# The shift of a softmax's scores: minima split in token layout, turned in f32r one step later, and written to the queries straight from PSUM

## The chip, the core and the metric

The kernel runs on one core of a Trainium2 chip. The metric is the time on the device in microseconds, the median of several executions. Matrix products run on TensorE (PE in the rows, its weight loads PEld), elementwise work on VectorE (DVE), ScalarE (ACT) and GpSimd (POOL); SyncE (SP) issues most DMAs. Every engine works through its own list of instructions in order, and engines wait for each other by semaphores.

## The reference

Two batches of 512 tokens of width 512 attend to 1,024 context tokens each, in 16 heads of 32. The first 257 context tokens ("image") and the other 767 ("text") have separate key and value weights and **separate softmaxes**, whose results are added:

```
q = rms_norm(linear(x, q_w, q_b)); k, k_img likewise from the context
img_x = softmax(q k_img^T / sqrt(32)) v_img
txt_x = softmax(q k^T / sqrt(32)) v
x = x + linear(txt_x + img_x, o_w, o_b)
```

A feed-forward stage follows: the last token of each batch goes four times through a 512-2048-512 layer with GELU, and its result, under a sigmoid gate of every token, is added and normalised.

## The kernel before

**Units and steps.** Attention runs over 16 units: 2 halves of the queries x 2 batches x 4 groups of 4 heads, 256 queries each. A unit has 8 steps of 128 keys. The function `make_plan` (line 69) writes one list of steps out by hand, and every engine goes through it and does its own part of each; so the list sets the order on all engines. In step r of the loop of line 247 TensorE does

- `S2(r)`: scores of step r with the keys on partitions and 4 x 256 (head, query) columns, four f32r products (line 837);
- `PV(r-1)`: probabilities times values of the step before, in f32 (line 856, with row sums on line 861);
- `S1(r+12)`: scores of a unit one and a half ahead, now with the queries on partitions, two f32r products of 512 columns (line 820). They serve to find maxima alone. VectorE reduces them to negated maxima `negt` (lines 1273 and 1275); three PSUM banks take turns.

In between stand pieces of the rest: output projection (`o`), the feed-forward chain (`ch_...`), the gate (`f_...`).

**The shift.** exp needs the scores less a maximum per query, head and softmax. The maximum is added inside S2: the operands `kst` and `qst` have 112 rows, of which 96 hold keys and queries (split in high and low f32r parts) and 16 hold, in `kst`, ones at the right (head, image or text) and in `qst` the negated maxima, in 8 rows the high and in 8 the low part. They get there so:

1. `maxes(u)`, VectorE (line 1279): two small minima over the partial results give `negm`, 128 queries x 16, the 8 values twice, in f32.
2. `shift(u)`, TensorE (line 881): two f32 products with the identity turn it to 16 x 256 in rows 96 to 111 of a PSUM bank.
3. `shift(u)`, ScalarE (line 1102): copy to `crow` in f32r, which rounds to the high part. `shift(u)`, VectorE (line 1298): high rows stay, low rows become value minus high part, by a column `lows` of 0 and -1 that a DMA brings.
4. `spread(u)`, ScalarE (line 1108): the 16 rows are copied to the four heads of `qst`.

Units are counted from 0 in the code (u) and from the first in the text: the ninth unit is u = 8. The minima and the shift of unit u stand in step 4 of unit u-1, that is between S1 and the next S2, and the spread in step 5; S2 of unit u needs them three steps later. Unit 0 is done in the first phase, between the value projections.

## Time and profile before

| | |
|---|---|
| median of 3 runs | 564.36 us (559.66 to 565.49) |
| the profiled execution's own time | 565.07 us |
| its span, first to last instruction | 563.2 us |
| TensorE busy, of the span | 519.2 us, 92% |
| VectorE, ScalarE, GpSimd busy | 64%, 55%, 41% |
| mean granted TensorE clock | 0.969 |

The first 155 us are projections, the last 45 us gate and output; between them the 16 units run at 17.5 us each where nothing else stands among their steps. The page gives shares of the whole span. What a change inside a unit is worth is read from the timeline of one step: which engine another one waits for there, and how far apart the groups of one engine start.

### The profile page before, as it was taken

What the parts mean: (1) busy time and instruction counts of PE and PEld (TensorE: products, weight loads), DVE (VectorE), ACT (ScalarE), POOL (GpSimd) and SP (SyncE); (2) the same over time, 40 slices, a digit from 0 to 9 for tenths busy, and PEclk for the clock granted to TensorE, in tenths of its full rate; (3) what the DMA queues carried; (4) which work ended last, traced back from release to release, by engine and by line L of the source; (5) the groups of instructions that cost most, each with busy time, mean ns of one, the idle gap of its engine ahead of it and who ended that gap; (6) DMA issues with size and microseconds to landing.
All of it is one profiled execution on the core that took longest, in us unless ns stands there. A gap on an engine that the chain in (4) does not pass through costs nothing.

```text
span 563.2 us, 9907 instructions
## 1 busy us (share of the span) xinstructions
PE 519.2 (92%) x3800; PEld 318.4 (57%) x3800; DVE 358.9 (64%) x760; ACT 310.3 (55%) x556; POOL 233.5 (41%) x140
## 2 busy tenths in 40 slices
PE   4999999599898999999999999999999999998970
PEld 3888879477664555555556454445454545554430
DVE  4388666667676478567766687384747375439565
ACT  4874367232265466446666364657474646767432
POOL 1230022220075385545546427070716164849531
PEclk9999999889999799999999997999999999999995
DMA  8977379829889969746777685425242363000101
GB/s 297 402 224 275 149 169 259 236 84 309 221 246 278 219 154 245 200 133 174 201 202 199 127 225 162 126 57 127 57 127 58 125 189 118 2 20 19 39 19 56
DMA packets 61328, 91.92 MB, mean 163 GB/s; under 512 B 4513, under 2 KB 29105, under 8 KB 60705
## 3 DMA queue, kind: packets, MB, share of 16 engines
q1 hardware_dynamic: 56848, 74.68, 47.8%
q0 software_dynamic: 3312, 14.51, 7.8%
q10 hardware_dynamic: 1120, 2.10, 1.3%
q8 instruction: 30, 0.49, 0.4%
q14 instruction: 18, 0.14, 0.1%
HBM read 71.87 MB, written 19.66 MB: 163 GB/s over the span
## 4 chain that ended last, share of the span: by engine, by line
PE 67%; DVE 15%; DMA 8%; ACT 4%; POOL 3%; issue 3%; SPq 0%; POOLq 0%; DVEq 0%; ACTq 0%
PE psum L747 12%; PE psum L856 11%; PE psum L820 10%; PE psum L837 9%; PE psum L861 6%; PE psum L895 5%; DMA qscr<-hl 3%; DVE negt L1275 3%; PE psum L932 3%; DVE negt L1273 2%; PE psum L756 2%; PE psum L952 2%; DMA qst<-qscr 2%; PE psum L988 2%; PE psum L884 2%
## 5 line engine op out<-in xcount | busy, mean ns | idle before, releaser
L1090 ACT ACTIVATE prob<-psum 128x512 f32<-128x512 f32 x256 | 138.5, 593 | 99.4 <-PE psum L837 97.2
L1275 DVE TENSOR_REDUCE negt<-psum 128x1 f32<-128x512 f32 (+1 forms) x256 | 134.9, 548 | 55.0 <-PE psum L820 54.7
L1505 POOL TENSOR_TENSOR added<-added,prob 128x1024 f32<-128x1024 f32 x48 | 114.2, 2380 | 14.8 <-ACT prob L1090 9.5
L820 PE MATMUL psum<-kst,qst 96*128 96x512 f32 x256 | 98.9, 462 | 12.8 <-DVE negt L1275 9.2
L1502 POOL TENSOR_TENSOR added<-prob 128x1024 f32<-128x1024 f32 x16 | 38.0, 2372 | 154.6 <-ACT prob L1090 154.6
L837 PE MATMUL psum<-qst,kst 112*128 112x256 f32 x512 | 94.0, 301 | 1.2 <-ACT prob L1090 0.8
L837 PEld LDWEIGHTS psum<-qst,kst 112*128 112x128 f32 x512 | 77.8, 192 | 28.3 <-ACT prob L1090 10.2
L856 PE MATMUL psum<-prob,vring 128*32 128x256 f32 x1152 | 90.7, 397 | 0.0
L820 PEld LDWEIGHTS psum<-kst,qst 96*128 96x128 f32 x256 | 40.7, 190 | 66.9 <-issue 36.8
L1273 DVE TENSOR_REDUCE negt<-psum 128x1 f32<-128x257 f32 x128 | 53.0, 414 | 30.4 <-PE psum L820 30.3
L1455 POOL TENSOR_TENSOR ssum<-sq 128x512 f32<-128x512 f32 x6 | 8.6, 1439 | 80.1 <-ACT sq L1055 63.8
L861 PE MATMUL psum<-prob,ones 128*32 128x256 f32 x512 | 36.9, 383 | 0.0
L856 PEld LDWEIGHTS psum<-prob,vring 128*32 128x32 f32 x1152 | 24.7, 109 | 20.7 <-issue 1.1
L1054 ACT ACTIVATE raw<-psum,colp 128x512 f32<-128x512 f32 (+2 forms) x32 | 19.1, 596 | 29.7 <-PE psum L747 28.3
L747 PE MATMUL psum<-p_wv,tok 128*128 128x512 f32 x144 | 34.4, 392 | 0.0
L988 PE MATMUL psum<-wg,xTt 128*128 128x512 f32 x64 | 30.2, 607 | 0.6 <-ACT xTt L1158 0.6
L747 PEld LDWEIGHTS psum<-p_wv,tok 128*128 128x128 f32 x144 | 26.9, 188 | 5.9 <-issue 0.2
L895 PE MATMUL psum<-wbuf,attT 128*128 128x512 f32 x64 | 29.4, 601 | 0.4 <-issue 0.4
L747 PE MATMUL psum<-tok,p_wk 128*128 128x256 f32 (+1 forms) x144 | 25.9, 331 | 0.0
L1072 ACT ACTIVATE vbuf<-psum 128x512 f32<-128x512 f32 x14 | 8.4, 598 | 29.6 <-PE psum L747 29.5
L747 PEld LDWEIGHTS psum<-tok,p_wk 128*128 128x128 f32 x144 | 22.2, 198 | 2.4
L747 PE MATMUL psum<-tok,p_wq 128*128 128x512 f32 x96 | 23.5, 400 | 0.0
(159 smaller groups left out, 683.5 us busy)
## 6 DMA issues: line engine op xcount, KB each, us to landing
kst<-kscr SPq DMA_DIRECT2D x96, 256.0 KB, 5.7
vring<-vscr SPq DMA_DIRECT2D x16, 576.0 KB, 7.0
kscr<-hl SPq DMA_DIRECT2D x16, 512.0 KB, 2.9
d<-d POOLq DMA_DIRECT2D x8, 1024.0 KB, 6.9
qst<-qscr SPq DMA_DIRECT2D x48, 128.0 KB, 5.6
vscr<-vbuf SPq DMA_DIRECT2D x18, 256.0 KB, 2.7
qscr<-hl SPq DMA_DIRECT2D x8, 512.0 KB, 5.0
in_c<-ctxT SPq DMA_DIRECT2D x2, 1024.0 KB, 12.4
```

Of the source, the lines that this page charges most:

```text
L747: mm = pe.matmul(ps, left(a, kc), right(b, kc), start=(kc == 0 and a + b == 0), stop=(kc == KC - 1 and a == 1))
L820: pe.matmul(psum[:, n % 3, :], qst[0:96, slot, jj, qt * P:(qt + 1) * P], kst[0:96, slot, jj, half * 512:(half + 1) * 512], start=True, sto ...
L837: mm = pe.matmul(score2[:, j * QH:(j + 1) * QH], kst[0:96 + 4 * HPG, slot, jj, k0:k0 + P], qst[0:96 + 4 * HPG, slot, jj, :], start=True, s ...
L856: mm = pe.matmul(psum[32 * j:32 * j + 32, PV_BANK, st * QH:(st + 1) * QH], vring[:, u % 2, vc, 32 * j:32 * j + 32], prob[:, r % NP, j * QH ...
L861: mm = pe.matmul(psum[32 * j:32 * j + 32, SUM_BANK, st * QH:(st + 1) * QH], ones[:, kind, :], source[:, j * QH:(j + 1) * QH], start=first, ...
L895: mm = pe.matmul(ps, attT[:, g, n * P:(n + 1) * P], wbuf[:, g, :], start=(g == 0), stop=(g == NG - 1))
L988: mm = pe.matmul(ps, xTt[:, f % 2, kc, :], wg[:, kc, :], start=(kc == 0), stop=(kc == KC - 1))
L1090: act.activation(prob[:, r % NP, part], score2[:, part], ACT.Exp).then_inc(exp2_done, 1)
L1273: dve.tensor_reduce(negt[:, u % 2, qt, 0, j:j + 1], psum[:, n % 3, 0:IMG], AX.X, ALU.max, negate=True)
L1275: dve.tensor_reduce(negt[:, u % 2, qt, half, HPG + j:HPG + j + 1], psum[:, n % 3, k0:512], AX.X, ALU.max, negate=True)\
L1502: pool.tensor_tensor(added[:, :], prob[:, (r - 1) % NP, :], prob[:, r % NP, :], ALU.add).then_inc(added_done, 1)
L1505: pool.tensor_tensor(added[:, :], added[:, :], prob[:, r % NP, :], ALU.add).then_inc(added_done, 1)
```

## The change

- The negated maxima are split where the queries are still on partitions. `maxes` writes the high part to `negm`, now f32r and 112 columns wide (columns 0 to 95 are zero, written once), then the value and the negated high part to `negp`, and their sum as low part to `negm`: four small instructions, the third and fourth each waiting for one before it.
- TensorE turns `negm` with an f32r identity, so that its 112 columns are the weights and the output takes rows 0 to 111.
- The ScalarE copy to `crow` and VectorE's subtraction go; `spread` reads PSUM itself. The bank is free when `spread` is done.
- In the loop `shift` stands one step later, between S2 and PV.
- The DMA of `lows` goes; a copy makes the f32r identity in unit 0.

```diff
     for r in range(8 * NU + 2):
         if r < 8 * NU:
             add('S2', r)
+            if (r + ahead) % 8 == 1 and r + ahead <= 8 * NU + 1:
+                add('shift', (r + ahead) // 8 - 1)
...
         if t < 8 * NU:
             add('S1', t)
-        if t % 8 == 0 and t <= 8 * NU:
-            add('shift', t // 8 - 1)
...
-        negm = sb("negm", [P, 2, 2, 4 * HPG], F32, o); o += 256
+        negp = sb("negp", [P, 2, 2 * HPG, 2], F32, o); o += 128
+        identr = sb("identr", [P, P], F32R, o); o += 512
...
-        crow = sb("crow", [P, 2, QH], F32R, arena + 43 * KB_)
+        negm = sb("negm", [P, 2, 2, 96 + 4 * HPG], F32R, arena + 43 * KB_)
...
-                    mm = pe.matmul(ps[96:96 + 4 * HPG, qt * P:(qt + 1) * P], negm[:, u % 2, qt], ident[:, :], start=True, stop=True)
+                    mm = pe.matmul(ps[0:96 + 4 * HPG, qt * P:(qt + 1) * P], negm[:, u % 2, qt], identr[:, :], start=True, stop=True)
...
-            def shift(u):
-                job = job_at[('shift', u)]
-                act.wait_ge(job_done, job + 1)
-                rows_of = slice(96, 96 + 4 * HPG)
-                act.copy(crow[rows_of, 0, :], psum[rows_of, bank_of[job], 0:QH]).then_inc(shift_high, 1)
-
             def spread(u):
                 slot = pair_slot(u, 0)[0]
+                job = job_at[('shift', u)]
                 rows_of = slice(96, 96 + 4 * HPG)
-                act.wait_ge(shift_low, u + 1)
+                act.wait_ge(job_done, job + 1)
                 act.copy(qst[rows_of, slot:slot + 2].rearrange("p a b n -> p (a b) n"),
-                         crow[rows_of, 1, :].rearrange("p (o n) -> p o n", o=1).to_broadcast([4 * HPG, 4, QH])).then_inc(shift_written, 1)
+                         psum[rows_of, bank_of[job], 0:QH].rearrange("p (o n) -> p o n", o=1).to_broadcast([4 * HPG, 4, QH])).then_inc(shift_written, 1)
...
             def maxes(u):
                 dve.wait_ge(max_done, 16 * (u + 1))
-                for qt in range(2):
-                    twice = negt[:, u % 2, qt].rearrange("p (o s) j -> p o j s", o=1).to_broadcast([P, 2, 2 * HPG, 2])
-                    ins = dve.tensor_reduce(negm[:, u % 2, qt].rearrange("p (o j) -> p o j", o=2), twice, AX.X, ALU.min)
-                ins.then_inc(negm_done, 1)
+                if u == 0:
+                    dve.tensor_copy(identr[:, :], ident[:, :])
+                    dve.memset(negm[:].bitcast(F32), 0.0).then_inc(negm_order, 1)
+                    dve.wait_ge(negm_order, 1)
+                high = negm[:, u % 2, :, 96:96 + 2 * HPG]
+                both = negt[:, u % 2].rearrange("p q s j -> p q j s")
+                dve.tensor_reduce(high, both, AX.X, ALU.min).then_inc(negm_order, 1)
+                dve.tensor_reduce(negp[:, :, :, 0], both, AX.X, ALU.min)
+                dve.wait_ge(negm_order, 2 + 2 * u)
+                dve.tensor_reduce(negp[:, :, :, 1], high.rearrange("p q (j o) -> p q j o", o=1), AX.X, ALU.min, negate=True).then_inc(negm_order, 1)
+                dve.wait_ge(negm_order, 3 + 2 * u)
...
+                    dve.tensor_reduce(negm[:, u % 2, :, 96 + 2 * HPG:96 + 4 * HPG], negp[:], AX.X, ALU.add).then_inc(negm_done, 1)
...
-            def shift(u):
-                job = job_at[('shift', u)]
-                if u > 0:
-                    dve.wait_ge(shift_written, u)
-                dve.wait_ge(shift_high, u + 1)
-                rows_of = slice(96, 96 + 4 * HPG)
-                dve.scalar_tensor_tensor(crow[rows_of, 1, :], crow[rows_of, 0, :], lows[rows_of, 0:1],
-                                         psum[rows_of, bank_of[job], 0:QH], ALU.mult, ALU.add).then_inc(emptied_by['dve'], 1)
-                dve.wait_ge(emptied_by['dve'], emptied(job)[1])
-                dve.engine_nop().then_inc(shift_low, 1)
```

**TensorE, around the second unit's shift, before** (`kst,qst` is S1 and `qst,kst` is S2, `vring` is PV, `negm` the shift):

```order
L856 MATMUL psum<-prob,vring 32x256 x4
L820 MATMUL psum<-kst,qst 128x512 x2
L884 MATMUL psum<-ident,negm 16x128 x2
L837 MATMUL psum<-qst,kst 128x256 x4
L856 MATMUL psum<-prob,vring 32x256 x4
L820 MATMUL psum<-kst,qst 128x512 x2
```

The same place in the changed kernel:

```order
L855 MATMUL psum<-prob,vring 32x256 x4
L819 MATMUL psum<-kst,qst 128x512 x2
L836 MATMUL psum<-qst,kst 128x256 x4
L883 MATMUL psum<-identr,negm 112x128 x2
L855 MATMUL psum<-prob,vring 32x256 x4
L819 MATMUL psum<-kst,qst 128x512 x2
```

The shift has changed places with the four products of S2; it now stands between two groups of different type, f32r before it and f32 behind it.

**VectorE, around the second unit's minima, before** (`negt<-psum` are the maxima of S1):

```order
L1273 TENSOR_REDUCE negt<-psum 128x1
L1275 TENSOR_REDUCE negt<-psum 128x1
L1282 TENSOR_REDUCE negm<-negt 128x16 x2
L1275 TENSOR_REDUCE negt<-psum 128x1 x2
L1304 SCALAR_TENSOR_TENSOR crow<-crow,lows,psum 16x256
```

The same place in the changed kernel:

```order
L1269 TENSOR_REDUCE negt<-psum 128x1
L1280 TENSOR_REDUCE negm<-negt 128x2x8
L1281 TENSOR_REDUCE negp<-negt 128x16
L1283 TENSOR_REDUCE negp<-negm 128x16
L1286 TENSOR_REDUCE negm<-negp 128x2x8
L1269 TENSOR_REDUCE negt<-psum 128x1 x8
```

Four instructions stand where two stood, and the one behind the next two maxima is gone.

## Rows read from the trace of the kernel before

**Rows 1.** The page: span, engines, and the granted clock in 40 slices.

```profile
span 563.2 us, 9907 instructions
...
PE 519.2 (92%) x3800; PEld 318.4 (57%) x3800; DVE 358.9 (64%) x760; ACT 310.3 (55%) x556; POOL 233.5 (41%) x140
...
PEclk9999999889999799999999997999999999999995
```

**Rows 2.** Groups by line: busy us, mean ns of one | idle before.

```profile
L837 PEld LDWEIGHTS psum<-qst,kst 112*128 112x128 f32 x512 | 77.8, 192 | 28.3 <-ACT prob L1090 10.2 <-issue 10.0 <-ACT vbuf L1072 0.7
```

**Rows 3.** Timeline around the ninth unit's shift: start us, us, engine, line [idle before <-releaser].

```profile
297.11 7.41 POOL L1505 TENSOR_TENSOR added<-added,prob 128x1024 f32<-128x1024 f32 x3
...
297.27 0.73 PE L820 MATMUL psum<-kst,qst 96*128 96x512 f32 x2
...
297.83 0.64 PE L837 MATMUL psum<-qst,kst 112*128 112x256 f32 x4
...
298.40 0.64 PE L856 MATMUL psum<-prob,vring 128*32 128x256 f32 x8
...
298.97 0.73 PE L820 MATMUL psum<-kst,qst 96*128 96x512 f32 x2
299.25 0.28 DVE L1282 TENSOR_REDUCE negm<-negt 128x16 f32<-128x32 f32 x2
...
299.65 0.34 PEld L884 LDWEIGHTS psum<-ident,negm 128*16 128x16 f32 x4 [0.38 <-issue]
...
300.21 0.74 PE L837 MATMUL psum<-qst,kst 112*128 112x256 f32 x4
...
300.83 0.49 DVE L1304 SCALAR_TENSOR_TENSOR crow<-crow,lows,psum 16x256 fp32r<-16x256 f32 x1
...
300.88 0.64 PE L856 MATMUL psum<-prob,vring 128*32 128x256 f32 x8
...
305.60 0.61 PE L861 MATMUL psum<-added,ones 128*32 128x256 f32 x8
```

**Rows 4.** One tile's instructions (negm): ns min/median/max.

```profile
L884 PEld LDWEIGHTS psum<-ident,negm x64: 92/94/151, 144.4 to 487.5; 128*16 128x16 f32 x64
...
L1282 DVE TENSOR_REDUCE negm<-negt x32: 174/182/190, 144.0 to 487.0; 128x16 f32<-128x32 f32 x32
```

**Rows 5.** Timeline, VectorE, 5 us earlier: the second waits for the first.

```profile
294.01 0.41 DVE L1293 TENSOR_TENSOR pvc<-pvc,psum 128x256 f32<-128x256 f32 x1
...
294.45 0.48 DVE L1295 SCALAR_TENSOR_TENSOR attT<-psum,vbias,pvc 128x256 f32<-128x256 f32 x1
```

**Rows 6.** Timeline, the fourth unit's minima and shift.

```profile
203.71 0.28 DVE L1282 TENSOR_REDUCE negm<-negt 128x16 f32<-128x32 f32 x2
...
204.14 0.60 PE L884 MATMUL psum<-ident,negm 128*16 128x128 f32 x4
```

**Rows 7.** Timeline, the fifteenth unit's minima and shift.

```profile
462.90 0.28 DVE L1282 TENSOR_REDUCE negm<-negt 128x16 f32<-128x32 f32 x2
...
463.33 0.60 PE L884 MATMUL psum<-ident,negm 128*16 128x128 f32 x4
```

**Rows 8.** Timeline: the fourth unit's first score product waits for its queries.

```profile
182.89 0.73 PE L820 MATMUL psum<-kst,qst 96*128 96x512 f32 x2 [2.37 <-DMA qst<-qscr]
```

**Rows 9.** Timeline around the eleventh unit's shift, at the lower clock.

```profile
345.61 1.22 PE L820 MATMUL psum<-kst,qst 96*128 96x512 f32 x2
...
348.88 1.08 PE L856 MATMUL psum<-prob,vring 128*32 128x256 f32 x8
```

**Rows 10.** Windows: us, busy of PE, PEld, DVE, ACT, POOL, PEclk, DMA share, GB/s.

```profile
183.90:190.70 6.80, 6.80 (x45) 3.72 (x42) 2.59 (x5) 3.58 (x6) 4.16 (x3) 0.51 1.13 247
```

**Rows 11.** Timeline behind the sixteenth unit's shift: ScalarE and TensorE.

```profile
488.89 0.36 ACT L1106 CAST crow<-psum 16x256 fp32r<-16x256 f32 x1
...
489.28 1.08 ACT L1090 ACTIVATE prob<-psum 128x512 f32<-128x512 f32 x2
...
490.50 0.80 PE L837 MATMUL psum<-qst,kst 112*128 112x256 f32 x2
```

More of the change, by code:

```diff
@@ L299 @@
 SPLIT_OF = {n: i for i, n in enumerate(SPLITS)}
-JOBS = {'xT': 'dve', 'proj': 'act', 'sumsq': 'act', 'v': 'act', 'vimg': 'act', 'shift': 'dve', 'o': 'dve',
+JOBS = {'xT': 'dve', 'proj': 'act', 'sumsq': 'act', 'v': 'act', 'vimg': 'act', 'shift': 'shift', 'o': 'dve',
         'ch_turn': 'dve', 'ch_agg': 'act', 'ch_d1': 'dve', 'ch_hT': 'act', 'ch_d2': 'act', 'ch_sum': 'act',
@@ L400, in build @@
         xterms = sb("xterms", [P, 2, 8], F32, o); o += 64
-        lows = sb("lows", [P, 1], F32, o); o += 32
         assert o % 32 == 0
@@ L473, in build @@
         job_done = sem("job_done")
-        emptied_by = {'act': sem("emptied_by_act"), 'dve': sem("emptied_by_dve")}
+        shift_written = sem("shift_written")
+        emptied_by = {'act': sem("emptied_by_act"), 'dve': sem("emptied_by_dve"), 'shift': shift_written}
         sumsq_added = sem("sumsq_added")
@@ L485, in build @@
         negm_done = sem("negm_done")
-        shift_high = sem("shift_high")
-        shift_low = sem("shift_low")
-        shift_written = sem("shift_written")
+        negm_order = sem("negm_order")
         s2_done = sem("s2_done")
@@ L538, in v_stores @@
             return 16 * ((chunks - slot + 3) // 4)
-        n_const, n_rows = 3, 1 + 3 + 4 + 2
+        n_const, n_rows = 2, 1 + 3 + 4 + 2
         tok_of = {('k', 0, 0): 'c00', ('k', 0, 1): 'c01', ('k', 1, 0): 'c10', ('k', 1, 1): 'c11b'}
@@ L1179, in _ @@
                      'f_exp': f_exp, 'f_sig': f_sig, 'f_stat2': f_stat2, 'x_stat': x_stat,
-                     'shift': shift, 'spread': spread}
+                     'spread': spread}
             for e in plan:
@@ L1279, in maxes @@
                 dve.wait_ge(max_done, 16 * (u + 1))
-                for qt in range(2):
-                    twice = negt[:, u % 2, qt].rearrange("p (o s) j -> p o j s", o=1).to_broadcast([P, 2, 2 * HPG, 2])
-                    ins = dve.tensor_reduce(negm[:, u % 2, qt].rearrange("p (o j) -> p o j", o=2), twice, AX.X, ALU.min)
-                ins.then_inc(negm_done, 1)
+                if u == 0:
[9 more added lines that the diff above has]
+                dve.wait_ge(negm_order, 3 + 2 * u)
+                with nc.allow_low_precision(reason="the difference of two f32 values is exact here; it is stored as the low part"):
+                    dve.tensor_reduce(negm[:, u % 2, :, 96 + 2 * HPG:96 + 4 * HPG], negp[:], AX.X, ALU.add).then_inc(negm_done, 1)
             def weigh(u):
@@ L1426, in _ @@
             steps = {'consts': consts, 'split': split, 'xstat': xstat, 'xnorm': xnorm, 'xT': xT, 'norm': norm, 'S1': S1, 'maxes': maxes, 'weigh': weigh,
-                     'shift': shift, 'o': o, 'ch_stat': ch_stat, 'ch_ln': ch_ln, 'ch_turn': ch_turn, 'ch_agg': ch_agg,
+                     'o': o, 'ch_stat': ch_stat, 'ch_ln': ch_ln, 'ch_turn': ch_turn, 'ch_agg': ch_agg,
                      'ch_d1': ch_d1, 'ch_sum': ch_sum, 'ch_bc': ch_bc,
@@ L1443, in link @@
                 pool.wait_ge(pool_order, links[0])
-            for dst, src in ((colp[:], T['cols']), (lows[:, :], T['lows']), (ident[:, :], T['ident'])):
+            for dst, src in ((colp[:], T['cols']), (ident[:, :], T['ident'])):
                 pool.dma_start(dst, src).then_inc(const_loaded, 16)
@@ L1570 @@
     ind = ind.reshape(HPG, 4 * HPG, KEYS).transpose(1, 0, 2)
-    lows = np.zeros((P, 1), np.float32)
-    lows[96 + 2 * HPG:96 + 4 * HPG] = -1
     host = {
@@ L1583 @@
         'd1_b': get('L0_ffn_d1_b'),
-        'ident': eye, 'ind': ind, 'lows': lows, 'sel': np.tile(eye[:32, :32], (4, 1)),
+        'ident': eye, 'ind': ind, 'sel': np.tile(eye[:32, :32], (4, 1)),
     }
```

## The prediction

> **What bounds the kernel now.** I read the page first: TensorE is busy for 92% of the span, the others for 64% and less [rows 1]. That is an average, so the next view is the timeline of one step of an ordinary unit. The thing to see there is how far apart TensorE's groups start, not how long each is. S1 starts at 297.27, S2 0.56 us later at 297.83, PV 0.57 later at 298.40, the next S1 0.57 later at 298.97 [rows 3]. Each group follows as soon as the array can take it, so in the units TensorE's list is the path, and whatever sits in it is paid in full.
>
> The shift sits in it. From the S1 at 298.97 to the PV at 300.88 are 1.91 us, where the step before needed 298.40 - 297.27 = 1.13 [rows 3]. One shift costs 0.78 us, and fifteen of them stand in the loop: 11.7 us can be had at most.
>
> The same rows say what it is made of. The minima start at 299.25 and end at 299.53; the first weight load of the shift starts at 299.65, 0.12 later. So TensorE has stood since 298.97 + 0.56 = 299.53 and waited for VectorE, a little. From that load to S2 are 0.56 us, and from S2 to PV 0.67 instead of 0.57, since the array changes from the f32 product back to f32r. Counted from the start of the minima, n: the load at n + 0.40, S2 at n + 0.96, PV at n + 1.63. The waiting is the rule: from the minima to the shift's first product are 0.43 us in the fourth unit (203.71 to 204.14) and 0.43 in the fifteenth (462.90 to 463.33) [rows 6, 7]. Eleven shifts (units 4 to 10 and 12 to 15) have it.
>
> **VectorE's part.** Two instructions of 182 ns, with both ended 0.28 us after the first began, become four [rows 3, 4]. The first two wait for nothing in between: the first ends at n + 0.18 and the second at 0.28, as now. The third waits for the first. A waiting instruction starts 0.03 us behind the end of what it waits for: 294.01 + 0.41 = 294.42, and the next starts at 294.45 [rows 5]. So the third runs from 0.21, but hardly before the second is well under way, say 0.23, to 0.41, the fourth from 0.44 to 0.62. The minima are ready at n + 0.62 instead of n + 0.28. The bounds: 0.52, if the shorter input of the third makes it quicker, and 0.86, if all four go strictly one behind another (4 x 0.18 and four gaps). The maxima of the next S1 are queued behind them and start 0.34 later; the 0.49 us instruction on `crow` that stood behind these maxima [rows 3] is gone, so VectorE has caught up before the next S1 needs its bank. I cost that at nothing; its cover is the two steps in which VectorE has two maxima instead of four per step.
>
> **TensorE's part.** S2 moves in front of the wait. It starts at 298.97 + 0.56 = 299.53, its last product is issued by about 299.98, and the next group could start at 300.10. The minima are ready at 299.87, the load starts 0.12 later, at 299.99. From a load that nothing covers to the next group I have only the f32 case, 0.56. For the new pair, f32r with 128 moving columns, no row exists. It can be built from S2: its four products of 256 columns take 0.57 to the next group [rows 3], about 0.12 each and 0.10 for the change of type. Two products of half the columns, with weights loaded in the open, come to 0.22 for the first, 0.12 for the second (the load of 112 columns binds rather than the 128 moving ones) and 0.16 to the next group: 0.50. Bounds: 0.24, if a load is fully covered and only the products count, and 0.70, if the narrow f32r pair is worth as much as the f32 pair plus the wide load. I take 0.50, it being nearest to S2's own rows. PV then starts at 299.99 + 0.50 = 300.49 instead of 300.88: **0.39 us less per shift**. Not all of it is certain to survive (the ends of products are modelled in the trace); I take 0.37. For eleven shifts that is 4.1 us.
>
> Row against rule, on the wider weights: a single load of 16 columns takes 94 ns, one of 112 x 128 takes 192 [rows 2, 4], and before there were four narrow ones per shift where now two wide ones stand, 376 against 384 ns, so the width costs nothing in the sum. The Trainium skill, page "TensorE: Matmul & The Clock Gate", section on LDWEIGHTS, has a load cost its columns divided by 1.2 ns, whatever the rows. By that the loads would grow from 4 x 13 to 2 x 93 ns, 0.13 us per shift and 2.0 us for fifteen, and the sum below would come to 561.6 instead of 559.6. The trace does not agree for the narrow load, 94 ns for 16 columns.
>
> **The other shifts.** The third unit's and the eleventh's run where the granted clock is 0.51 or is about to fall to it, the lower level of 1.2 GHz [rows 10], and wait for no minimum: there the array is the bound. From S1 to PV the eleventh takes 348.88 - 345.61 = 3.27 us [rows 9, 10]; at half clock a step without shift is twice 1.13, so the shift costs 1.0, and of that about half goes with the cheaper pair and the one change of type less: 0.5 to 0.6 each, 1.1 together. The second unit's shift comes before the place where the fourth unit's first score product waits 2.37 us for its queries [rows 8]. That DMA is held by other transfers rather than by TensorE, so what is gained before it turns into a longer wait: 0. For the same reason I cost the first unit's extras (an identity copy, a memset, the longer chain, under 1 us, between projections) at nothing.
>
> **The last shift** has ScalarE behind it. TensorE's S2 at 490.50 waits for the exp that runs from 489.28 to 490.37, and in front of that exp stands the copy to `crow`, 0.36 us [rows 11]. It goes, so this S2 comes 0.37 earlier. Elsewhere the same copy and the spread's new source are idle time of ScalarE, which waits for TensorE in nearly every step. GpSimd's sum of probabilities ends at 297.11 + 7.41 = 304.52 and TensorE reads it at 305.60 [rows 3]; 0.37 us earlier still leaves 0.7.
>
> **The sum.** 4.1 + 1.1 + 0.37 = 5.5 us less than the profiled execution's 565.07: **559.6 us**. The median of the three runs is 564.36, 0.7 below that execution; against it the gain would end at 558.8.
>
> **The rivals.**
>
> *The narrow f32r pair is dear.* Each product of 128 moving columns takes as long as the f32 pair it replaces, 0.22 us instead of 0.12. For it: no f32r product with fewer than 256 moving columns is among the rows, so nothing shows that the rate holds there. Against it: 512 and 256 columns scale cleanly. It adds 0.2 us to each of 15 shifts, 3.0 in all: 562.6. The page's rule on loads leads to nearly the same place, 561.6; I give both together 0.25.
>
> *The chain of minima becomes the wait (slower).* S2 covers the chain only so far. With PV at n + X + 0.12 + 0.50 against n + 1.63 now, the change loses from X = 1.01 on, that is with each of the four instructions at 0.25 us. If a write to an f32r tile followed by a dependent read of few elements cost 0.35 us each, X would be 1.4, each of 13 shifts 0.4 later, and the kernel at 570.3. Against it: 182 ns and 0.03 us gaps in the rows. Chance 0.04.
>
> *Clock.* The page's clock row dips in three places between its ends [rows 1]. One of them is the 6.8 us from 183.9 with 0.51 granted and TensorE busy throughout [rows 10], right behind the 2.37 us in which it waited for queries [rows 8]. Such a stretch costs 6.8 x 0.49 = 3.3 us. If the moved work takes one away, 556.3; if it brings one, 562.9. The three runs before span 5.8 us, so one comes or goes already. Chance 0.10 for fewer, 0.08 for more.
>
> *It changes nothing.* TensorE is let go by something else at each step, and gives the time back: 565. The strict spacing in rows 3 speaks against it. Chance 0.06.
>
> The forecast itself has 0.47.
>
> **Range and chances.** From 555.0 (one slow stretch fewer and a shift that is fully covered in some units) to 564.5 (dear pair, or one slow stretch more, with a little noise): this leaves out about 2 in 10. About 1% is what can be told from no change here, 5.6 us, or 558.7 against the median. The forecast ends at its edge, so it gives half of its 0.47 less a bit to faster (0.20), with the whole of the fewer-stretches case (0.10) and a part of the others where pairs are cheap (0.07): 0.37. Slower by over 1%: the chain, and a slow stretch on top of no gain: 0.06. The rest, 0.57, within 1%.
>
> **What would show it.** Right: PV begins 1.5 us after the S1 in the shift's step (1.91 before); the fourth small VectorE instruction ends 0.6 us after the first begins; the weight load of the shift begins 0.1 us behind it, with S2 complete in front of it; ordinary units last 17.1 instead of 17.5 us. Wrong: two products of the shift starting 0.2 us apart (dear pair); the chain over 1 us long; or S1 of the following steps starting as late as before with an idle reason of its own. The prediction fails most easily on the price of the pair, and on the number of slow-clock stretches, which is not the change's doing.

## The result and the profile after

| | before | after |
|---|---|---|
| runs, median (range) | 563.85 us (559.66 to 565.49, 4) | 556.18 us (554.97 to 557.39, 4) |
| the profiled execution's own time | 565.07 us | 557.1 us |
| its span | 563.2 us | 555.2 us |
| mean granted TensorE clock | 0.969 | 0.976 |

The ratio of the runs is 0.990, with an interval of 0.985 to 0.994: about 1% faster. The forecast was 559.6 us, from 555.0 to 564.5. Medians and ranges here and below are over all executions; ratios leave out the few that took over 1.5% more than the fastest of their kernel.

The page of the changed kernel, to be set against [rows 1]:

```profile
span 555.2 us, 9813 instructions
...
PE 510.0 (92%) x3768; PEld 319.2 (57%) x3768; DVE 354.8 (64%) x778; ACT 303.7 (55%) x540; POOL 234.1 (42%) x139
```

TensorE keeps its share of 92% of a shorter span, so it is still the path. The number to read is where the shift sits. The timeline around the ninth unit's shift, columns as in [rows 3]:

```profile
297.35 0.73 PE L819 MATMUL psum<-kst,qst 96*128 96x512 f32 x2
297.63 0.19 DVE L1280 TENSOR_REDUCE negm<-negt 128x16 fp32r<-128x32 f32 x1
...
297.74 0.17 DVE L1281 TENSOR_REDUCE negp<-negt 128x16 f32<-128x32 f32 x1
297.85 0.17 DVE L1283 TENSOR_REDUCE negp<-negm 128x16 f32<-128x16 f32 x1
297.92 0.64 PE L836 MATMUL psum<-qst,kst 112*128 112x256 f32 x4
298.06 0.19 DVE L1286 TENSOR_REDUCE negm<-negp 128x16 fp32r<-128x32 f32 x1
...
298.37 0.27 PEld L883 LDWEIGHTS psum<-identr,negm 128*112 128x112 f32 x2
298.40 0.38 PE L883 MATMUL psum<-identr,negm 128*112 128x128 f32 x2
...
298.71 0.64 PE L855 MATMUL psum<-prob,vring 128*32 128x256 f32 x8
...
299.28 0.74 PE L819 MATMUL psum<-kst,qst 96*128 96x512 f32 x2
```

S2 now follows S1 by 0.57 us, in front of the shift, and VectorE's four small instructions run while S2 does. From S1 to PV are 298.71 - 297.35 = 1.36 us, where [rows 3] had 1.91. From S1 to the next S1 are 1.93 us; a step without a shift takes 1.71. The shift costs 0.2 us instead of 0.76 ([rows 3], S1 to S1): 0.55 saved. The chain of minima takes 298.06 + 0.19 - 297.63 = 0.62 us, and the weight load begins 0.12 us behind its end.

The loads of the wide `negm` (one tile's instructions, ns min/median/max, against [rows 4]):

```profile
L883 PEld LDWEIGHTS psum<-identr,negm x32: 172/176/309, 146.4 to 480.2; 128*112 128x112 f32 x32
```

What the change costs is in the first phase. The timeline of the changed kernel at the first unit's minima:

```profile
144.95 0.23 DVE L1275 CAST identr<-ident 128x128 fp32r<-128x128 f32 x1
145.22 0.43 DVE L1276 MEMSET negm<- 128x448 f32 x1
...
146.11 0.19 DVE L1286 TENSOR_REDUCE negm<-negp 128x16 fp32r<-128x32 f32 x1
...
146.45 0.61 PE L883 MATMUL psum<-identr,negm 128*112 128x128 f32 x2 [1.63 <-DVE negm L1286]
```

TensorE stands 1.63 us here. Before, the same place reads:

```profile
144.39 0.60 PE L884 MATMUL psum<-ident,negm 128*16 128x128 f32 x4 [0.57 <-DVE negm L1282]
```

So the identity copy, the memset and the longer chain make this wait 1.06 us longer. Whether all of that reaches the end of the kernel is another question, taken up below.

**Two quantities come and go from run to run.** One is the lower clock of 1.2 GHz: outside the last 30 us, the trace before has 20.5 us of it (three stretches of 6.8), the one after 13.7. The other is the wait of the fourth unit's first score product for its queries, 2.37 us before [rows 8] and 1.56 after. Half of the former and all of the latter are taken off each span in this table; "rest" is an estimate of what the kernel itself takes. To take the wait off as well was decided after the traces were there.

| profiled execution | span | lower clock, us | wait for queries | rest |
|---|---|---|---|---|
| before | 563.2 | 20.5 | 2.37 | 550.6 |
| before, again | 564.9 | 17.1 | 5.03 | 551.3 |
| changed | 555.2 | 13.7 | 1.56 | 546.8 |
| changed, again | 557.8 | 17.1 | 4.87 | 544.4 |
| only the order | 553.3 | 10.2 | 2.68 | 545.5 |
| only the order, again | 554.4 | 13.7 | 2.41 | 545.2 |
| only the split | 567.3 | 27.3 | 3.25 | 550.4 |
| narrow | 556.3 | 23.9 | 2.00 | 542.3 |
| narrow, again | 558.1 | 27.3 | 2.15 | 542.3 |

The two traces of before are 0.7 us apart in "rest", those of the changed kernel 2.4, though their spans are 1.7 and 2.6 apart. Means: 551.0 and 545.6, a gain of 5.4 us.

**The same from all executions.** Every execution has its mean granted clock on record. Within one kernel the span falls by 0.44 us for each 0.001 more of it, and that takes up about three quarters of the scatter (190 executions, the long ones left out). With this slope the mean span of each kernel can be put to one clock, 0.974. The kernels of the lower rows are those of the experiments:

| kernel | executions | mean clock | mean span at 0.974, us (95% interval, by resampling) |
|---|---|---|---|
| before | 84 | 0.9754 | 561.7 (561.5 to 561.9) |
| changed | 16 | 0.9725 | 554.9 (554.4 to 555.4) |
| only the order | 15 | 0.9757 | 555.4 (554.7 to 556.2) |
| only the split | 12 | 0.9675 | 562.1 (561.4 to 562.8) |
| extras early | 9 | 0.9688 | 554.7 (554.2 to 555.1) |
| narrow | 18 | 0.9713 | 554.3 (553.9 to 554.7) |
| pair twice | 10 | 0.9732 | 557.7 (557.0 to 558.4) |
| longer chain | 9 | 0.9710 | 560.8 (560.3 to 561.4) |
| shorter chain | 11 | 0.9698 | 557.4 (556.9 to 557.9) |
| narrow, extras early | 6 | 0.9717 | 554.3 (553.2 to 555.1) |

At one clock the change gains 6.8 us (6.2 to 7.4), so the clock did not make the difference.

### The profile page after: what moved, and what is told of

It reads as the page before. It is cut to its first block, busy times and chain, and to the rows that moved or that the text cites. A ratio compares the mean times of both kernels' runs of the same rounds, so it can differ in the third digit from the quotient of the medians.

```text
span 555.2 us, 9813 instructions
## 1 busy us (share of the span) xinstructions
PE 510.0 (92%) x3768; PEld 319.2 (57%) x3768; DVE 354.8 (64%) x778; ACT 303.7 (55%) x540; POOL 234.1 (42%) x139
## 4 chain that ended last, share of the span: by engine, by line
PE 72%; DVE 10%; DMA 8%; ACT 4%; POOL 4%; issue 2%; SPq 1%; POOLq 0%; DVEq 0%; ACTq 0%
PE psum L746 13%; PE psum L819 12%; PE psum L855 12%; PE psum L836 10%; PE psum L860 6%; PE psum L894 5%; DMA qscr<-hl 4%; PE psum L931 3%; PE psum L951 2%; PE psum L755 2%; DMA qst<-qscr 2%; PE psum L987 2%; POOL added L1497 1%; DMA kscr<-hl 1%; DVE negt L1269 1%
## 5 line engine op out<-in xcount | busy, mean ns | idle before, releaser
L819 PE MATMUL psum<-kst,qst 96*128 96x512 f32 x256 | 98.9, 462 | 12.9 <-DVE negt L1269 10.2
L836 PE MATMUL psum<-qst,kst 112*128 112x256 f32 x512 | 91.7, 296 | 1.3 <-ACT prob L1089 1.0
L855 PE MATMUL psum<-prob,vring 128*32 128x256 f32 x1152 | 89.1, 391 | 0.0
L746 PE MATMUL psum<-p_wv,tok 128*128 128x512 f32 x144 | 36.7, 411 | 0.0
L746 PEld LDWEIGHTS psum<-p_wv,tok 128*128 128x128 f32 x144 | 28.7, 201 | 6.2
```

What stands on the lines that cost most here:

```text
L746: mm = pe.matmul(ps, left(a, kc), right(b, kc), start=(kc == 0 and a + b == 0), stop=(kc == KC - 1 and a == 1))
L819: pe.matmul(psum[:, n % 3, :], qst[0:96, slot, jj, qt * P:(qt + 1) * P], kst[0:96, slot, jj, half * 512:(half + 1) * 512], start=True, sto ...
L836: mm = pe.matmul(score2[:, j * QH:(j + 1) * QH], kst[0:96 + 4 * HPG, slot, jj, k0:k0 + P], qst[0:96 + 4 * HPG, slot, jj, :], start=True, s ...
L855: mm = pe.matmul(psum[32 * j:32 * j + 32, PV_BANK, st * QH:(st + 1) * QH], vring[:, u % 2, vc, 32 * j:32 * j + 32], prob[:, r % NP, j * QH ...
```

## The experiments

All are compared with the kernel before on the same chip. The theory: S2 covers the wait for the minima, and a cheaper f32r pair adds to it. The rivals: the pair is dear; the order alone does it; the split alone does it; the clock made the difference.

**Only the order.** The kernel before, with `shift` behind S2 and nothing else changed.

```diff
             add('S2', r)
+            if (r + ahead) % 8 == 1 and r + ahead <= 8 * NU + 1:
+                add('shift', (r + ahead) // 8 - 1)
...
-        if t % 8 == 0 and t <= 8 * NU:
-            add('shift', t // 8 - 1)
```

> The kernel before with one edit: the shift stands behind S2 instead of in front of it. It still is an f32 pair, copied by ScalarE and split by VectorE. Theory (the gain is made inside the step of the shift, of S2 covering the wait and of the cheaper pair): the minima are ready 0.28 us after their start n, S2 covers that, the pair starts at n + 0.85 and PV at about n + 1.4 instead of n + 1.63, so the step from S1 to PV lasts 1.65 us instead of 1.91, and fifteen shifts give 3.5 to 4 us: ratio about 0.994. Rival (the gain of 7.7 us is mostly one or two stretches at the lower clock that come and go): the step may shorten, but the time follows the number of such stretches, anything from 556 to 566.

Measured: 556.45 us (552.36 to 559.78, 6 runs) against 563.86, ratio 0.988 (0.984 to 0.993). The order alone gives as much as the whole change, within the noise: at one clock it gains 6.3 us (5.5 to 7.0), where 3.5 to 4 were expected, and the changed kernel is 0.5 ahead of it (from 0.4 behind to 1.4 ahead). Its timeline around the ninth unit's shift:

```profile
295.55 0.73 PE L820 MATMUL psum<-kst,qst 96*128 96x512 f32 x2
295.84 0.28 DVE L1282 TENSOR_REDUCE negm<-negt 128x16 f32<-128x32 f32 x2
...
296.12 0.64 PE L837 MATMUL psum<-qst,kst 112*128 112x256 f32 x4
...
296.69 0.28 PE L884 MATMUL psum<-ident,negm 128*16 128x128 f32 x1
...
296.70 0.42 PE L856 MATMUL psum<-prob,vring 128*32 128x256 f32 x3
...
296.81 0.38 PE L884 MATMUL psum<-ident,negm 128*16 128x128 f32 x2
...
297.14 0.59 PE L856 MATMUL psum<-prob,vring 128*32 128x256 f32 x2
...
297.66 0.73 PE L820 MATMUL psum<-kst,qst 96*128 96x512 f32 x2
```

The minima end at 296.12, when S2 begins, so nothing waits for them. PV begins 0.01 us behind the shift's first product, and the two groups alternate in the trace: 16-column f32 products between the 32-column ones of PV. The step is 2.11 us, a shift 0.40: 0.36 below before, 0.18 above the changed kernel. Of the changed kernel's 0.55 us in an ordinary step, then, 0.36 are the order's and 0.18 the split's with its f32r pair. In the sixth and the tenth unit it is the other way round: 3.81 us from S1 to S1 before, 3.01 with the order alone, 3.27 in the changed kernel.

**Only the split.** The changed kernel, with `shift` in front of S2 as before.

```diff
-            if (r + ahead) % 8 == 1 and r + ahead <= 8 * NU + 1:
-                add('shift', (r + ahead) // 8 - 1)
...
+        if t % 8 == 0 and t <= 8 * NU:
+            add('shift', t // 8 - 1)
```

> The changed kernel with one edit undone: the shift stands in front of S2 again. Theory: TensorE now waits in the open for the longer chain of minima (ready at n + 0.61), so the load is at n + 0.72, S2 at about n + 1.0 and PV at n + 1.6: almost all of the gain in the step is lost, S1 to PV 1.85 to 1.9 us, and the kernel is at 562 to 565, ratio 0.997 to 1.002. Rival (the pair and the instructions saved on ScalarE and VectorE make the gain, the place does not matter): 556 to 558.

Measured: 566.3 us (563.85 to 571.54, 12), ratio 1.006 (1.003 to 1.009). Its timeline around the ninth unit's shift:

```profile
303.81 0.73 PE L819 MATMUL psum<-kst,qst 96*128 96x512 f32 x2
...
304.82 0.27 PEld L883 LDWEIGHTS psum<-identr,negm 128*112 128x112 f32 x2 [0.71 <-issue]
304.85 0.39 PE L883 MATMUL psum<-identr,negm 128*112 128x128 f32 x2 [0.31 <-DVE negm L1286]
...
305.07 0.69 PE L836 MATMUL psum<-qst,kst 112*128 112x256 f32 x4
...
305.69 0.64 PE L855 MATMUL psum<-prob,vring 128*32 128x256 f32 x8
...
306.26 0.30 PEld L819 LDWEIGHTS psum<-kst,qst 96*128 96x128 f32 x2 [0.41 <-DVE negt L1269]
```

In front of S2 the longer chain is paid in full: the load begins 0.73 us behind the start of the minima instead of 0.40. The load to S2 takes 0.25 instead of 0.56 [rows 3]. The two cancel, S1 to S1 is 2.45 against 2.47, and the split by itself gains nothing. The ratio of 1.006 is above the range expected: these executions had a mean clock of 0.9675, and at one clock the kernel is level with the one before (562.1 against 561.7). By these rows the split can pay only where something covers its chain.

**The changed kernel again**, to see what repeats.

> The changed kernel again, untouched, for the spread of its times and for a second trace: which of its stretches at the lower clock come again. Theory: step of the shift 1.36 us as in the first trace, 555 to 558 us, ratio 0.985 to 0.99; the lower clock behind the first unit's shift (145.7 to 152.5 in the first trace) comes again, since TensorE waits 1.6 us there for the first unit's minima in every run. Rival (luck): that stretch is gone, or another one stands in the units as in the kernel before.

Measured: 557.37 us (553.68 to 561.56, 12), ratio 0.991 (0.988 to 0.994). The steps are the same to 0.02 us (1.92). The lower clock is not: stretches of 3.4 and 6.8 us (length, busy of PE, PEld, DVE, ACT, POOL, granted clock, DMA share, GB/s) of the first trace of the changed kernel,

```profile
145.70:152.50 6.80, 6.05 (x15) 4.83 (x16) 3.54 (x9) 0.12 (x1) 0.00 (x0) 0.52 0.64 173
186.70:190.10 3.40, 3.40 (x19) 2.29 (x18) 1.76 (x3) 2.09 (x3) 3.26 (x3) 0.53 1.15 212
```

and of this one:

```profile
145.70:152.50 6.80, 5.68 (x26) 4.77 (x27) 5.17 (x12) 1.60 (x2) 0.00 (x0) 1.00 0.65 190
185.90:192.70 6.80, 5.85 (x30) 4.10 (x34) 2.58 (x4) 2.86 (x5) 3.25 (x3) 0.52 1.14 205
513.60:517.00 3.40, 2.56 (x25) 1.19 (x29) 1.33 (x1) 0.81 (x2) 3.40 (x3) 0.53 0.21 80
```

The same code has the low level at 145.7 once and not the other time, so the theory that the wait in front of it brings it in every run does not hold. Chance alone hardly explains the stretches either. Of all fourteen traces each has a low stretch from 109 to 112 us on, and twelve have one from 183 to 187 us on (behind the fourth unit's wait for queries, DMA share above 1). One from 146 to 150 us on, behind the first unit's shift, is in seven of the ten traces of kernels with the new arithmetic and in none of the four with the old. The mean clocks of the executions agree: 0.9755 with the old arithmetic (99 executions), 0.9708 with the new (91), 2.1 us at 0.44 us for each 0.001. The changed kernel by itself has 0.9725, about 1.3 us. So the rewritten arithmetic seems to have a price in clock that the order alone does not pay; what brings the stretch on was not tried.

**The extras of the first unit taken away.** The identity copy goes to the start of the program, the memset to GpSimd in an idle place.

```diff
+                dve.tensor_copy(identr[:, :], ident[:, :])   # in consts, at the start
...
                 if u == 0:
-                    dve.tensor_copy(identr[:, :], ident[:, :])
-                    dve.memset(negm[:].bitcast(F32), 0.0).then_inc(negm_order, 1)
...
+            def zero():
+                pool.wait_ge(job_done, last_k + 1)
+                pool.memset(negm[:].bitcast(F32), 0.0).then_inc(negm_order, 1)
```

> The changed kernel, but the identity copy is made with the other constants at the start and GpSimd writes the zeros of negm some 10 us earlier, so that the first unit's minima follow the last maxima at once. Theory (the two extras on VectorE lengthen the first phase): TensorE's wait in front of the first unit's shift falls from 1.6 us by 0.7; if this is what lets the clock fall behind it, the 6.8 us stretch goes too and gives 3.4 more: 552 to 555.5, ratio 0.98 to 0.984. Rival (the first phase is late by a DMA, a store of keys for which VectorE waits): nothing, 556.

Measured: 559.38 us (554.62 to 561.5, 9), ratio 0.992 (0.989 to 0.995). In the trace the wait falls from 1.63 to 0.90 us:

```profile
145.40 0.38 PE L883 MATMUL psum<-identr,negm 128*112 128x128 f32 x2 [0.90 <-DVE negm L1285]
```

The remaining 0.33 above before are the longer chain. The time is above the 552 to 555.5 us expected, and the 0.7 us don't show: at one clock this kernel is 0.2 us ahead of the changed one (from 0.5 behind to 0.9 ahead). The low stretch from 146 us on came again here, though the wait in front of it was shorter (0.90 us).

**Narrow weights.** `negm` has 16 columns, the output goes to rows 0 to 15 of the bank, `spread` reads it there and writes rows 96 to 111.

```diff
-        negm = sb("negm", [P, 2, 2, 96 + 4 * HPG], F32R, ...)
+        negm = sb("negm", [P, 2, 2, 4 * HPG], F32R, ...)
...
-                    mm = pe.matmul(ps[0:96 + 4 * HPG, qt * P:(qt + 1) * P], negm[:, u % 2, qt], identr[:, :], start=True, stop=True)
+                    mm = pe.matmul(ps[0:4 * HPG, qt * P:(qt + 1) * P], negm[:, u % 2, qt], identr[:, :], start=True, stop=True)
```

> The changed kernel with negm 16 instead of 112 columns wide: the f32r pair loads 16 columns, its output lies in PSUM rows 0 to 15, and ScalarE's spread reads it there and writes rows 96 to 111. Theory (the loads start while S2 still runs, so width is hidden or costs as little as the rows of before say, 94 against 192 ns): load 0.09 us instead of 0.18, step from S1 to PV 1.30 to 1.36 us against 1.36, under 1 us in the whole. Rival (the load's columns bind the pair, as in the rule that costs a load its columns divided by 1.2 ns): pair 0.06 us apart instead of 0.12, S1 to PV 1.2, 2 to 2.5 us less in all, 554 to 555.

Measured: 557.76 us (556.46 to 559.8, 8), ratio 0.989 (0.986 to 0.992). The load, and the ninth unit's shift:

```profile
L883 PEld LDWEIGHTS psum<-identr,negm x32: 92/93/143, 145.5 to 481.3; 128*16 128x16 f32 x32
```

```profile
296.25 0.72 PE L819 MATMUL psum<-kst,qst 96*128 96x512 f32 x2
...
297.30 0.28 PE L883 MATMUL psum<-identr,negm 128*16 128x128 f32 x2
297.51 0.64 PE L855 MATMUL psum<-prob,vring 128*32 128x256 f32 x8
298.08 0.74 PE L819 MATMUL psum<-kst,qst 96*128 96x512 f32 x2
```

The step is 1.83 us against 1.93: the 112 columns cost 0.10 per shift in ordinary units, and nothing in the twelfth to fourteenth (5.66 us both). At one clock the kernel is 0.6 us ahead of the changed one (0.0 to 1.3). The ends of the products are modelled; the starts are what to read.

**The pair twice.** Each product of the shift is issued two times.

```diff
-                for qt in range(2):
+                for qt in (0, 1, 0, 1):
```

> The changed kernel with the shift's two f32r products issued twice (the same result). It prices the pair. Theory (a narrow f32r product costs its load distance, 0.12 us): each shift 0.24 us longer, S1 to PV 1.6, 15 shifts 3.6 us, 560 to 561. Rival of the prediction (128 moving columns run at the f32 rate): 0.44 us, 6.5 us in all, 563 to 564.

Measured: 560.12 us (556.49 to 563.62, 10), ratio 0.994 (0.991 to 0.998).

```profile
296.31 0.72 PE L819 MATMUL psum<-kst,qst 96*128 96x512 f32 x2
...
297.35 0.58 PE L883 MATMUL psum<-identr,negm 128*112 128x128 f32 x4
297.86 0.64 PE L855 MATMUL psum<-prob,vring 128*32 128x256 f32 x8
298.43 0.74 PE L819 MATMUL psum<-kst,qst 96*128 96x512 f32 x2
```

The step grows from 1.93 to 2.12: 0.19 for two products with their loads, 0.10 each. The rival of the dear pair, 0.22 each, falls. In the twelfth to fourteenth unit it is only 0.05 (5.71 against 5.66). With 0.19 in the other twelve shifts that makes 2.4 us, and it arrives in the end: 2.8 us at one clock (1.9 to 3.7).

**A longer chain.** The third small instruction is done three times, each waiting for the one before.

```diff
+                for n in range(2):
+                    dve.tensor_reduce(negp[:, :, :, 1], ..., ALU.min, negate=True).then_inc(negm_order, 1)
+                    dve.wait_ge(negm_order, 4 + n + 4 * u)
```

> The changed kernel with two more dependent small instructions among VectorE's minima (the third is done three times). The minima take 1.0 to 1.05 us instead of 0.61. Theory (S2 covers the chain of 0.61 us to within 0.03 us, any more stands in the open on TensorE): all 0.4 us show in each of the fifteen shifts but the third unit's, S1 to PV 1.76 us, 5 to 6 us in all, 562 to 564, and perhaps a further stretch at the lower clock behind a longer wait. Rival (there is slack of some tenths in front of PV): 558 to 560.

Measured: 564.55 us (560.98 to 570.69, 10), ratio 1.002 (0.998 to 1.005): the gain is gone. Around the ninth unit's shift:

```profile
303.69 0.72 PE L819 MATMUL psum<-kst,qst 96*128 96x512 f32 x2
303.97 0.19 DVE L1280 TENSOR_REDUCE negm<-negt 128x16 fp32r<-128x32 f32 x1
...
304.81 0.18 DVE L1289 TENSOR_REDUCE negm<-negp 128x16 fp32r<-128x32 f32 x1
...
305.14 0.38 PE L883 MATMUL psum<-identr,negm 128*112 128x128 f32 x2 [0.26 <-DVE negm L1289]
305.45 0.16 PEld L855 LDWEIGHTS psum<-prob,vring 128*32 128x32 f32 x8
```

The trace is that of the longest execution, but the granted clock is 1.00 around this step. The chain is 1.02 us, 0.40 longer, and the step 2.33, 0.40 longer. So at 0.62 the chain had used up S2's cover: what is added to it is paid at once. It arrives too: 15 x 0.40 = 6.0 us by the steps, 5.9 at one clock (5.2 to 6.8).

**A shorter chain.** The third instruction goes; the fourth subtracts the high part from the value, with two inputs.

```diff
-                dve.tensor_reduce(negp[:, :, :, 1], ..., ALU.min, negate=True).then_inc(negm_order, 1)
...
-                    dve.tensor_reduce(negm[..., low], negp[:], AX.X, ALU.add).then_inc(negm_done, 1)
+                    dve.tensor_tensor(negm[..., low], negp[:, :, :, 0], high, ALU.subtract).then_inc(negm_done, 1)
```

> The changed kernel with three instead of four small instructions: high part, value, and the low part as one subtraction of the two. The minima take 0.45 to 0.5 us instead of 0.61. Theory: ordinary units gain at most 0.03 us, since S2 covers the rest, but where the minima start late (the units with the output projection and with the feed-forward chain, where order alone left the step 0.10 to 0.26 us shorter than the whole change does) the 0.13 shows: 6 shifts, 0.8 us, plus 0.13 in the first unit; ratio 0.985 to 0.99 with the clock's spread on it. Rival: nothing to be seen.

Measured: 561.54 us (557.2 to 566.2, 12), ratio 0.995 (0.992 to 0.998), which is worse than the changed kernel (2.5 us at one clock), where 0.985 to 0.99 was expected. Usually the chain is 0.49 us and the step 1.86, 0.06 less: 0.13 off the chain buys only that, as TensorE is then the bound. But the two-input instruction has a tail, in the trace of that tile and in the timeline of the second unit (with GpSimd's sum beside it):

```profile
L1284 DVE TENSOR_TENSOR negm<-negp,negm x16: 174/242/2200, 145.5 to 479.5; 128x16 fp32r<-128x16 f32 x16
...
  PE psum L883: 6.4, 5
```

```profile
163.44 4.87 POOL L1495 TENSOR_TENSOR added<-added,prob 128x1024 f32<-128x1024 f32 x2
...
166.14 2.20 DVE L1284 TENSOR_TENSOR negm<-negp,negm 128x16 fp32r<-128x16 f32 x1
...
168.48 0.39 PE L883 MATMUL psum<-identr,negm 128*112 128x128 f32 x2 [1.74 <-DVE negm L1284]
```

It ends at 168.34, when GpSimd's instruction ends (163.44 + 4.87 = 168.31). TensorE's 6.4 us in five places are not all of this kind: 1.52 us are the first unit's, with its extras and no addition beside it, and 0.31 us follow an instruction that took 0.17. Three instructions that were held made TensorE wait 1.74, 1.12 and 1.67 us.

Which instructions are held can be read off the trace. In nine of the sixteen places the two-input instruction began while an addition of GpSimd was running. In eight of them it took 0.31 to 2.20 us and ended 0.03 to 0.04 us after the addition; in the ninth the addition was over 0.07 us later, and it took 0.17. In six it began 0.05 to 0.08 us before the addition and took 0.17 to 0.18, as here in the ninth unit; in one there was no addition.

```profile
296.66 0.17 DVE L1284 TENSOR_TENSOR negm<-negp,negm 128x16 fp32r<-128x16 f32 x1
```

```profile
296.74 2.38 POOL L1495 TENSOR_TENSOR added<-added,prob 128x1024 f32<-128x1024 f32 x1
```

The changed kernel's last reduction, with one input, took 0.19 us in all sixteen places, in fourteen of which it began while an addition ran.

**Narrow and extras away, together.**

```diff
+                dve.tensor_copy(identr[:, :], ident[:, :])   # in consts, at the start
...
-                    dve.memset(negm[:].bitcast(F32), 0.0).then_inc(negm_order, 1)
```

> The changed kernel with negm 16 columns wide, as in the narrow variant before it, so that no zeros have to be written, and with the identity copy made at the start. Theory: the two gains add up: 0.10 us in each ordinary shift (1.0 to 1.3 us), and 0.7 us less waiting at the first unit's shift, against the changed kernel; 554.5 to 556.5, ratio 0.983 to 0.988, with the profiled span less half of its microseconds at the lower clock 1.5 to 3 us under the changed kernel's 548.4 and 549.3. Rival (the first phase is bound by a store of keys anyway, and the clock's stretches hide the rest): 557 to 558, no faster than the narrow variant.

Measured: 557.11 us (554.66 to 560.38, 6), ratio 0.991 (0.987 to 0.994). The step is 1.83 and the wait at the first shift 0.91, both as in the two single edits. The measure that was announced, span less half of the lower-clock time, is 547.9 us, 0.5 and 1.4 below the changed kernel's two traces where 1.5 to 3 were expected. The "rest" is 543.1 us, some 2.5 below the changed kernel's mean, but 1.6 of that is the longer wait for queries taken off (4.79 us against 3.2 on average). At one clock it is 0.6 us ahead of the changed kernel (from 0.4 behind to 1.8 ahead).

**Three repetitions**: the kernel before with a profile of its own, the order alone, and the narrow kernel.

> The kernel before, untouched, for a second trace. Theory (a time is work plus half of the microseconds at the lower clock, and these come and go from run to run): span less half of the lower-clock time comes to 553 us again, within 1 us, whatever the span is. Rival (the lower clock belongs to the kernel): the same three stretches of 6.8 us in the same places.

> The kernel before with the order alone changed, a second time, beside the narrow variant on the same chip. By the steps of the traces it should lose against the narrow variant: 0.28 us more in each of seven ordinary shifts, 0.10 less in each of four in the feed-forward units, and about 1 us less in the first phase, since its minima there have no extras: some 0.5 to 1 us behind, which five rounds hardly tell. Rival: it is the fastest of all, as its first comparison (0.988) has it, by 1 us or more; then something that the steps do not show, such as the clock, favours it.

> The changed kernel with 16 columns of negm, a second time, beside the order alone. Expected at 0.985 to 0.989 of the kernel before, 0.5 to 1 us in front of the order alone; rival: behind it.

Measured: before, one execution, 566.66 us, step 2.48, wait for queries 5.03. Both accounts fail here. Span less half of the lower-clock time is 564.9 - 8.5 = 556.4, not 553 within 1; the longer wait for queries, 2.7 us more, is most of the difference. And the low stretches are not the same three: they start at 111, 183 and 251 us, where the first trace has 109, 184 and 344. Order alone 556.22 us (553.69 to 559.24, 9), ratio 0.990 (0.987 to 0.993). Narrow 557.59 us (553.43 to 559.92, 10), ratio 0.990 (0.987 to 0.994), where 0.985 to 0.989 was expected. By these ratios the two cannot be told apart, nor either from the changed kernel (0.990 and 0.991). At one clock, with the first runs of both, the narrow kernel is 1.1 us ahead of the order alone (0.3 to 2.0), about as the steps had it; in the plain medians its lower clock hides that.

## Why the prediction was right, and where it was not

**Right: the path and its cover.** TensorE's list is the path, S2 in front of the wait covers it, and what is added to a step arrives in the end (2.8 and 5.9 us where the steps had 2.4 and 6.0). PV was to begin 1.5 us behind S1; it is 1.36. The chain was to be 0.62; it is 0.62. The load was to begin 0.1 behind it; 0.12. Ordinary units, read from the starts of S1 eight steps apart, were to last 17.1 us instead of 17.5; they last 16.94.

**Mis-sized: the pair.** "Load in the open to the next group" was taken at 0.50 us, built from S2's rows; it is 298.71 - 298.37 = 0.34. The first product was put at 0.22 for an open load, but it begins 0.03 behind the load, and the pair twice shows 0.10 per product: 0.03 + 0.20 leaves 0.11 to the next group, where 0.16 were set. The saving per shift is therefore 0.55 instead of 0.37 in units 4 to 10 and 15. In units 12 to 14 it is 0.41 (6.07 to 5.66 us from S1 to S1): there the minima start later, 0.45 us behind the S1 in the twelfth unit instead of 0.28. For these eleven: 8 x 0.55 + 3 x 0.41 = 5.6 us instead of 4.1. The eleventh shift, costed at half clock, ran at the full clock in the second trace of before: 6.07 us there, 5.77 in the changed kernel, 0.3 saved. The third unit can't be read cleanly, since the clock changed there. The 0.10 us that the working gave to a change of type is shown by no run; with an f32r pair in front of S2 (only the split) S2 to PV is 0.62 us, where it was 0.67.

**Right in size, not in cause: the last shift.** From the last S1 to the S2 behind the exp (at 490.50 in [rows 11]) are 6.31 us before and 5.77 in the changed kernel: 0.5 saved, where 0.37 were forecast for the copy that goes. But with the split alone, where the copy is gone too, it is 6.29, and with the order alone, which keeps the copy and does it behind the exp, 5.66. So the order did it, and the near size is luck.

**Not settled: the first unit's extras at nothing.** They make TensorE wait 1.06 us longer. The working had that hidden by the later wait for queries. In the changed trace, with 6.8 us of lower clock besides, the first phase ends 4.5 us later (the first S2 begins at 159.77 against 155.23; 1.0 of it was there before the extras), and that wait takes back only 2.37 - 1.56 = 0.8 of it. Yet with the extras away the kernel is only 0.2 us faster at one clock (from 0.5 slower to 0.9 faster), where the wait was 0.7 shorter. The queries arrive between 181.9 and 187.5 us in the traces that show this wait; what sets that moment is open. What the term did leave out is the low stretch behind this shift, which came with the new arithmetic in seven of ten traces.

**Wrong: the width of the weights at nothing.** The comparison of 376 with 384 ns set four narrow loads against two wide ones, but the narrow f32r pair has two loads of 93 ns, and 0.10 us per shift is what the narrow experiment measured. The Trainium skill, page "TensorE: Matmul & The Clock Gate", section on LDWEIGHTS, has a load cost its columns divided by 1.2 ns. By that 96 more columns would be 80 ns a load. The measured loads differ by 176 - 93 = 83 ns, which agrees, while 16 columns take 93 and not 13: the slope holds here, with some 80 ns on top at either width.

**The sum.** Terms as measured: 5.6 + 0.5 + 0.3 for the eleventh unit + 0.55 for the third (an estimate, the ordinary saving) make 7.0 us, or 5.9 if all of the first unit's 1.1 is paid. All executions at one clock give 6.8 us (6.2 to 7.4); the "rest" of the traces gives 5.4, with 2.4 between two traces of one kernel. So the forecast's 5.5 was too small by about 1.3 us, which is the pair's term (4.1 where 5.6 came), partly offset by the third and eleventh units' 1.1, which came to 0.85. The time of 559.6 was too high by 3.4 us: besides the smaller gain, it was counted from an execution at a clock of 0.969, while the four of the changed kernel had 0.9755, worth some 2.9 us. That the time still lies in the range is in part luck: the range reached down to 555.0 for another reason, a low stretch fewer. Of the 8.0 us between the two profiled spans 3.4 are the lower clock's (6.8 us less of it, the rival of fewer stretches, beside the forecast) and 0.8 the wait for queries. The repetition (0.991, some 5 us) had the clock against it: 0.9715 for the changed kernel, 0.9748 for the one before.

**Wrong in emphasis: what the change is.** Most of the working went to the f32r pair and the chain. The order alone gives 0.988 and 0.990, the split alone 1.006. Where S2 covers the wait, the split's 0.18 us in an ordinary step is spent again elsewhere: in units 12 to 14 (5.66 against 5.56 us for the order alone), in the eleventh (5.77 against 5.55), the sixth and the tenth (3.27 against 3.01), and in part in the first. That the old pair would be cheap beside PV was not foreseen.

**The slower rival** had its point of decision at a chain of 1.01 us. At 1.02 the step is 2.33 us against 2.47, still 0.14 ahead, so the point lies near 1.16; the whole kernel is about level at 1.02 (ratio 1.002; at one clock 0.9 us ahead of before). The mechanism is as described, the point a little further out, since the pair is cheaper.

**Open.** Why the granted clock falls where it does, and why its stretches (3.4, 6.8 or 10.2 us long) come and go, and why the kernels with the new arithmetic have more of them. How much of the first unit's extras reaches the end. What sets the moment at which the queries arrive.

## What to carry over

- Where the path's engine waits for a small result, first move independent work of that engine in front of the wait, and measure this alone: here it gave 6.3 of the 6.8 us, and the rewritten arithmetic as it stands none that can be told from noise (with narrow weights 1.1).
- A cover is used up to its length and no further: 0.40 us more of chain cost 0.40 us per step, 0.13 less brought back 0.06. Count what is due behind the moved wait before lengthening it.
- One-time work (an identity, zeros) lengthens a wait where the engine that does it is waited for (1.63 to 0.90 us without it). Whether that reaches the end is read from the runs: here it did not show.
- Where executions of one kernel scatter with the granted clock, compare kernels at one clock, from all executions. One trace each is not enough: two traces of the changed kernel, corrected, were still 2.4 us apart.

## What the hardware showed that was not expected

- Products of 16 weight columns that write rows 96 to 111 and products of 32 columns (PV), both f32, run beside each other: their groups begin 0.01 us apart and alternate, and together they take 0.97 us, from 296.69 to the next S1 at 297.66, where PV alone takes 0.57. The pair in f32r that writes rows 0 to 15 does not do so (PV begins 0.21 behind it). Whether the type or the rows make the difference was not tried.
- A VectorE instruction with two inputs in SBUF was held for up to 2.20 us, until a running GpSimd addition ended. The order of starts decides in this trace: in the nine places where the addition was already running it did not end before the addition did, and in the six where it began first it took 0.17 to 0.18 us. The Trainium skill, page "GPSIMD Engine Reference", section 1 (Specifications), has GpSimd's SBUF interfaces shared with VectorE, in contention with VectorE's instructions of two SBUF inputs. The eight held instructions agree with it, and so do the reductions with one input, which were not held.
- Two small reductions on VectorE that don't wait for each other start 0.11 us apart though each takes 0.19. Behind a wait, the next starts 0.03 to 0.04 us after the end of what it waits for (297.63 + 0.19 to 297.85, 297.85 + 0.17 to 298.06).
